# Attention masks written into PSUM by TensorE's four row groups, in place of masked maxima, minima and selects on the other engines

## What is computed

```
scores = einsum('bhqd,bhkd->bhqk', Q, K) / sqrt(16)
scores = where(mask, scores, -inf)       # a mask per layer, below
attn   = softmax(scores); out = einsum('bhqk,bhkd->bhqd', attn, V) @ Wo
```

## Time and profile before

| | |
|---|---|
| median of 3 runs | 1161.6 us (1161.47 to 1162.02) |
| profiled execution: device time | 1159.94 us |
| profiled execution: span | 1157.7 us |
| TensorE (PE) busy | 1106.9 us, 96% |
| VectorE (DVE) busy | 841.3 us, 73% |
| ScalarE (ACT) busy | 618.6 us, 53% |
| GpSimd (POOL) busy | 258.8 us, 22% |

### The profile page before, as it was taken

One profiled execution on the slowest core, in us unless ns is written; L12 is line 12 of the kernel. 1 busy time (PEld: TensorE's weight loads), 2 busy tenths in 40 slices (PEclk: granted clock), 3 DMA queues, 4 the chain that ended last, 5 costly groups with the idle time before them and its releaser, 6 DMA issues. The chain is left out here.

```text
span 1157.7 us, 36414 instructions
## 1 busy us (share of the span) xinstructions
PE 1106.9 (96%) x13908; PEld 921.1 (80%) x13908; DVE 841.3 (73%) x3468; ACT 618.6 (53%) x1584; POOL 258.8 (22%) x383
## 2 busy tenths in 40 slices
PE   6999999999999999999999999999999999999886
PEld 5878778888778788878888887888888878787665
DVE  4466987957878687697687777786778685987841
ACT  3644455455555556545556565655556455545453
POOL 0322412203121230222304032320321223121100
PEclk9999999999999999999999999999999999999997
DMA  9600010200111001010010202001010100110000
GB/s 339 246 11 2 2 48 11 84 20 2 28 40 28 39 16 52 2 41 26 16 52 2 66 2 66 2 16 52 16 52 2 52 2 2 52 47 7 2 6 10
DMA packets 21224, 45.11 MB, mean 39 GB/s; under 512 B 2496, under 2 KB 14912, under 8 KB 18112
## 3 DMA queue, kind: packets, MB, share of 16 engines
q1 hardware_dynamic: 19952, 41.36, 10.1%
q10 hardware_dynamic: 1104, 1.44, 0.4%
HBM read 40.70 MB, written 2.10 MB: 37 GB/s over the span
## 5 line engine op out<-in xcount | busy, mean ns | idle before, releaser
L663 POOL TENSOR_TENSOR root<-var_eps,halves 128x1 f32<-128x1 f32 x128 | 76.9, 602 | 609.9 <-DVE var_eps L1171 588.1
L971 ACT ACTIVATE exps_t<-bank 128x512 f32<-128x512 f32 x256 | 135.7, 605 | 34.3 <-PE bank L795 33.8
L1111 DVE CUSTOM_DVE_ANT_0 bank<-bank,bias 128x128 f32<-128x128 f32 x512 | 130.1, 324 | 18.8 <-PE bank L763 18.8
L721 PE MATMUL bank<-x_t,weights_A 128*128 128x128 f32 x1024 | 139.3, 284 | 2.7 <-ACT x_t L931 2.1
L721 PEld LDWEIGHTS bank<-x_t,weights_A 128*128 128x128 f32 x1024 | 127.3, 197 | 12.1 <-ACT x_t L931 4.5
L721 PE MATMUL bank<-x_t,weights_F 128*128 128x128 f32 x1024 | 127.9, 281 | 2.8 <-ACT x_t L931 1.7
L721 PEld LDWEIGHTS bank<-x_t,weights_F 128*128 128x128 f32 x1024 | 121.6, 195 | 9.1 <-ACT x_t L931 3.1
L808 PE MATMUL bank<-exps_t,v_one 128*32 128x128 f32 x3072 | 114.5, 277 | 8.2 <-DVE exps_t L1083 6.1
L714 PE MATMUL bank<-weights_F,exps_t 128*128 128x256 f32 x512 | 121.1, 383 | 0.2 <-DVE neg_max L1111 0.2
L763 PE MATMUL bank<-k_eo,q_t 32*128 32x256 f32 x1536 | 107.7, 396 | 2.6 <-issue 1.7
L1111 DVE DVE_READ_ACCUMULATOR2_ANT neg_max<- 128x1 f32 x768 | 106.5, 139 | 0.1
(11 more groups left out here) (112 smaller groups left out, 1964.8 us busy)
## 6 DMA issues: line engine op xcount, KB each, us to landing
weight<-in_fside SPq DMA_DIRECT2D x16, 1024.0 KB, 4.9
weights_A<-in_weights_A SPq DMA_DIRECT2D x4, 1028.0 KB, 15.3
weights_F<-in_weights_F SPq DMA_DIRECT2D x2, 2054.0 KB, 17.9
drop_raw<-in_drop SPq DMA_DIRECT2D x16, 256.0 KB, 5.3
x_hat<-in_x SPq DMA_DIRECT2D x16, 128.0 KB, 2.5
out<-x_sum SPq DMA_DIRECT2D x16, 128.0 KB, 1.7
ctx_t<-in_ctx_t SPq DMA_DIRECT2D x13, 128.0 KB, 3.0
rows_A<-in_rows_A SPq DMA_DIRECT2D x3, 512.0 KB, 15.4
```

The lines of the kernel that those rows point to most:

```text
L663: nc.gpsimd.tensor_tensor(root[x][:], var_eps[x][:], halves[:, e:e + 1], ALU.pow).then_inc(done["root"], 1)
L721: mm = nc.tensor.matmul(dst[:, 128 * f:128 * f + 128], w[:, c, 128 * f:128 * f + 128], tokens_t[:, c, :], start=(c == 0), stop=(c == KC - 1))
L971: nc.scalar.activation(dst, score_bank(x, "ST", s, j)[:], ACT.Exp, scale=DH ** -0.5).then_inc(done["exp"], 1)
L1111: ins = nc.vector.tensor_tensor_reduce(out=heads[:, n, :], in0=heads[:, n, :], in1=mask_bias(x, s), scale=-1.0, scalar=2.0 ** 126, op0=ALU ...
```

## The change

1. A new step `put_mask` writes a mask into four PSUM banks ahead of the scores: 16 bfloat16 products, 4 blocks of 32 mask rows times the 4 row groups, each with a 32 by 32 identity repeated for the 4 heads (128 columns). It stands ahead of both S and ST in A0, A2 and A5: 6 times per item. The mask rows lie in `causal_rows`, `pair_rows` (2 buffers, one raw buffer) and `sxs_rows`, each spread so that every row group has all four blocks.
2. A0's S also gets the key mask by four products of 512 columns, as A1 has it; both now read one tile `key_rows` for all items.
3. The masked maxima (L1111), the minima (L1083) and the select (L645) are gone: all stages take a plain maximum of four heads at once (the old L1116), and the product with V waits for the exponential alone.
4. At the start TensorE spreads the causal mask by 32 small products, which VectorE copies. x is loaded in the order of its first use, half of it from ScalarE's queue; a 256 KB broadcast of the key mask is replaced by a small tile. The item masks are loaded by eight transfers per item in place of two. The raw shared mask borrows the buffer of A3's byte mask, so the first load of A3's weights waits until VectorE has made `sxs_rows` (at F0's fold).
5. All order tables, PLACES included, are new.

```diff
-PRELOADED = {"S": ("A1",), "ST": ()}
-ADDED = ("A0", "A2", "A5")
+PRELOADED = {"S": ("A0", "A1", "A2", "A5"), "ST": ("A0", "A2", "A5")}
...
-12345112112332124001001124551111001122210200010202203000120100001023032323103000230330303010011011201124101000001221
...
+12435112212124110021100430022203111122220001100003403041212050201010210345204142411101444411554215415541521555000400
...
             def _(sp):
-                load_x(sp, 0)
+                for x in FIRST[::2]:
+                    load_x(sp, x)
                 load_keys(sp)
...
+                sp.wait_ge(sxs_made, 1)
+                load_weight(sp, WEIGHT_TURNS[0])
...
             def _(pe):
-                pe.wait_ge(const_made, 4)
+                pe.wait_ge(const_made, 5)
+                for a in range(4):
+                    for r, (by_key, left, right) in enumerate(((0, idb, causal), (1, causal, idb))):
+                        for j in range(GROUPS):
+                            mm = nc.tensor.matmul(banks[r][32 * j:32 * j + 32, 128 * a:128 * a + 128], left[:, 32 * a:32 * a + 32],
+                                                  right[:], start=True, stop=True)
+                mm.then_inc(causal_spread, 1)
+                pe.wait_ge(causal_made, 2)
...
+                    if s in ("A0", "A1"):
+                        pe.wait_ge(keys_made, 2)
+                        for j in range(GROUPS):
+                            nc.tensor.matmul(score_bank(x, "S", s, j)[:], idb[group_rows(j), 32 * j + x:32 * j + x + 1].broadcast_to([32, N]),
+                                             key_rows[group_rows(j), :].unsqueeze(1).broadcast_to([32, GH, N]), start=True, stop=True,
+                                             skip_group_check=True)
+                    if s in PRELOADED["ST"]:
+                        put_mask(x, "S", s, s != "A0")
...
+                def put_mask(x, kind, s, first):
+
+                    if s == "A5":
+                        pe.wait_ge(sxs_made, 1)
+                    elif s == "A2":
+                        pe.wait_ge(done["pairs"], nth(x, "pairs", "in"))
+                    rows_of = mask_rows(x, s, 1 if kind == "S" else 0)
+                    for a in range(4):
+                        for j in range(GROUPS):
+                            columns = score_bank(x, kind, s, j)[:].rearrange("p (n k) -> p n k", n=GH)[:, :, 32 * a:32 * a + 32]
+                            nc.tensor.matmul(columns, rows_of[group_rows(j), a, :],
+                                             idb[group_rows(j), 32 * j:32 * j + 32].unsqueeze(1).broadcast_to([32, GH, 32]),
+                                             start=(first and a == 0), stop=True, skip_group_check=True)
...
                 def outputs(x, s, j):
-                    made = "later" if s == "A0" else "keep" if s in ("A2", "A5") else "exp"
-                    pe.wait_ge(done[made], nth(x, made, s, j))
+                    pe.wait_ge(done["exp"], nth(x, "exp", s, j))
...
+                def pair_masks(x):
+
+                    dve.wait_ge(pairs_loaded, 128 * (PAIR_TURNS.index(x) + 1))
+                    if x >= PAIR_BUFFERS:
+                        dve.wait_ge(done["ST"], nth(x - PAIR_BUFFERS, "ST", "A2"))
+                    nc.vector.tensor_scalar(pair_rows[x % PAIR_BUFFERS][:], pair_raw[:], 0.0, MASKED, ALU.is_equal, ALU.mult
+                                            ).then_inc(done["pairs"], 1)
...
                 def group_max(x, s, j):
...
-                        for n in range(GH):
-
-                            ins = nc.vector.tensor_tensor_reduce(
-                                out=heads[:, n, :], in0=heads[:, n, :], in1=mask_bias(x, s), scale=-1.0,
-                                scalar=2.0 ** 126, op0=ALU.add, op1=ALU.min, accum_out=neg_max[x][:, j, n:n + 1])
-                        ins.then_inc(done["max"], 1)
-                        return
                     nc.vector.tensor_reduce(neg_max[x][:, j, :], heads, AX_X, ALU.max, negate=True
                                             ).then_inc(done["max"], 1)
```

More of the change, by code:

```diff
@@ L155, in vector_lane @@
                 yield "k_eo", ATTN[s]["feeds"]
-            if s in ("A2", "A5"):
-                yield from (("keep", s, j) for j in range(GROUPS))
             if ATTN[s]["feeds"] and ATTN[ATTN[s]["feeds"]]["b"]:
@@ L192, in pool_lane @@
     for s in STAGES:
-        if s == "A0":
-            yield from (("later", s, j) for j in range(GROUPS))
         for n in LNS_AFTER[s]:
@@ L331 @@
 OUT_AT, OUT_BEFORE = shared_places(OUT_PLACES, [b for b in SCALAR_ORDER if b[1] == "o_raw"])
+FIRST = [beat[0] for beat in TENSOR_ORDER if beat[1:] == ("xT", "A0") and beat[0] < SETS]
+PAIR_TURNS = [beat[0] for beat in SYNC_ORDER if beat[1] == "load_pairs"]
 WEIGHT_TURNS = [beat[0] for beat in SYNC_ORDER if beat[1] == "load_weight"]
@@ L450, in program @@
         first_loaded = sem("first_loaded")
-        pairs_loaded = [sem(f"pairs_loaded{x}") for x in range(PAIR_BUFFERS)]
+        pairs_loaded = sem("pairs_loaded")
+        keys_made = sem("keys_made")
+        causal_spread = sem("causal_spread")
+        causal_made = sem("causal_made")
         stored = sems("stored")
@@ L455, in program @@
         done |= {k: sem(f"done_{k}") for k in ("x_t", "square", "v_copy", "k_copy", "q_t", "m_t", "exp", "o_raw", "o_t", "h_t")}
[L456 removed]
+        done |= {k: sem(f"done_{k}") for k in ("pairs", "folded", "k_eo", "v", "times", "lower", "max", "high_low", "o_norm", "sum",
                                                "stats", "x_hat")}
[L458 to L460 removed]
+        done |= {k: sem(f"done_{k}") for k in ("root", "res")}
         high_made = sem("high_made")
@@ L518, in taken @@
             return done[taker[0]], nth(x, *taker)
-        def four(ap):
-            return ap.unsqueeze(1).broadcast_to([128, GH, 128])
         def slots(j):
@@ L537, in head, with mask_rows @@
             return 8 * (n // 2) + 2 * j + n % 2
-        def mask_bias(x, s):
-            m = ATTN[s]["mask"]
-            return sxs_bias[:] if m == 3 else bias[x][:, m, :]
+        def mask_rows(x, s, by_key):
+            masks = causal_rows if s == "A0" else sxs_rows if s == "A5" else pair_rows[x % PAIR_BUFFERS]
+            return masks[:, by_key]
         def whole(name, b):
@@ L779, in transposed_scores @@
                         return
+                    masked = s in PRELOADED["ST"]
+                    if masked:
+                        for j in range(GROUPS):
+                            free_bank((x, "ST", s), j)
+                        put_mask(x, "ST", s, True)
                     for n in range(GH):
                         for j in range(GROUPS):
-                            if n == 0:
+                            if n == 0 and not masked:
                                 free_bank((x, "ST", s), j)
                             mm = nc.tensor.matmul(score_bank(x, "ST", s, j)[:, 128 * n:128 * n + 128], k_eo[x][group_rows(j), n // 2, n % 2, :],
-                                                  q_t[x][group_rows(j), n // 2, :], start=(n == 0), stop=True,
+                                                  q_t[x][group_rows(j), n // 2, :], start=(n == 0 and not masked), stop=True,
                                                   skip_group_check=True)
@@ L922, in _ @@
                 act.dma_start(weights["A0"][:, 0:half], dram["weights_A0"][:, 0:half]).then_inc(first_loaded, 16)
+                for x in FIRST[1::2]:
+                    load_x(act, x)
                 act.dma_start(weights["A0"][:, half:], dram["weights_A0"][:, half:]).then_inc(stage_loaded["A0"], 16)
-                for x in range(3):
+                for x in FIRST[1::2]:
                     load_ctx(act, x)
@@ L1014, in _ @@
                                       ).then_inc(parity_made, 1)
+                dve.wait_ge(causal_spread, 1)
+                for r in range(2):
+                    nc.vector.tensor_copy(causal_rows[:, r].rearrange("p a n -> p (a n)"), banks[r][:]).then_inc(causal_made, 1)
+                dve.wait_ge(keys_loaded, 32)
+                nc.vector.tensor_scalar(key_rows[:], key_raw[:], 0.0, MASKED, ALU.is_equal, ALU.mult).then_inc(keys_made, 1)
+                nc.vector.tensor_scalar(key_cols[:], key_cols_raw[:], 0.0, MASKED, ALU.is_equal, ALU.mult).then_inc(keys_made, 1)
                 def fold_norm(x, s):
```

268 lines of the change are left out of this document (97 added, 171 removed).

## The result

| | before | after |
|---|---|---|
| median of the runs | 1161.6 us | 1144.95 us (1143.6 to 1147.0) |
| ratio after to before, 95% interval | | 0.9854 [0.9837, 0.987] |
| profiled execution: device time, span | 1159.94, 1157.7 us | 1147.0, 1145.2 us |

1.5% faster. I had forecast 0.4% slower, and the time lies under my range too.

The account below looks back on a forecast made before the run. TensorE, busy 96% of the span, was taken as the bound: 1159.94 + 29.3 us added work - 24.5 us recovered, plus 1.7 us from profile to median, gives 1166 us, 0.4% slower. Own range 1159 to 1175; 8-in-10 range 1149 to 1181.

Parts of the forecast that it names:

- The sum's first term: Work added on TensorE by 96 put_mask steps at 0.34 us each, taken from the shift step: 32.6 us.
- My lower bound: For one put_mask on TensorE: 0.22 us, since the key mask streams the same 2048 columns in that time.
- Entry price: First float32 step on row groups behind a full-array product costs about 0.1 us more; 6.8 us come back.
- My count of 107 and 39 steps: S and ST steps directly behind a full-array product: 107 before, 39 after; 68 x 0.1 us saved.
- Key masks: A0's key masks on TensorE, 16 times four products of 512 columns at 0.22 us: 3.5 us more.
- Middle: 80 to 1040 us: of TensorE's 20.4 us idle, 11 come back as VectorE is relieved; bounds 0 and 17.
- End: Last 117.7 us: 8 of 19.4 us idle come back, plus 3 us on the last F1 product's clock.
- Start: TensorE's 9.33 us wait for the first x: 2.5 us come back with lighter loads; bounds -1 and 4.
- A: Rival: relief of VectorE is larger than TensorE's added work, 38 us back, 1153 us; chance 0.31.
- B: Rival: A3's single weight buffer makes TensorE late by 3 us at each of five items, 1181 us; chance 0.06.
- C: Rival: mask products don't pack as the shift does, 0.50 us a step, 15 us more, 1181 us; chance 0.04.
- D: Rival: both sides cancel within 0.2% (2.3 us); 33 us come back or a put_mask costs 0.25 us; chance 0.19.

Follow-up runs that it names:

- e4: The changed kernel with the 16 products of each put_mask done twice: 1165.66 us, 1.0038 of before.
- e9: The changed kernel with a full-array product of zeros, one column, between each mask step and its S or ST: 1163.62 us, 1.0031 of before.
- e10: The changed kernel with a one-column product of zeros on 32 rows between each mask step and its S or ST: 1146.99 us, 0.9887 of before.
- e2: The kernel before with A0, A2 and A5 unmasked (plain maxima, no minima, no select), order tables unchanged: 1137.63 us, 0.9788 of before.
- e1: The changed kernel with the order tables and bank places of before, item masks made at F0: 1156.94 us, 0.9971 of before.
- e3: The changed kernel without its 96 put_mask steps (A2 and A5 unmasked, A0 with the key mask alone): 1128.72 us, 0.9717 of before.
- e7: The changed kernel with x loaded by SyncE alone, in the order of before: 1145.53 us, 0.9858 of before.
- e13: The changed kernel with 33 further bfloat16 products, results unused, in TensorE's empty first 9 us: 1140.79 us, 0.9824 of before.
- e14: The changed kernel unedited, on the same chip as e13: 1144.69 us, 0.9859 of before.

## Why the prediction was wrong

1. **The sum's first term, "96 x 0.34 = 32.6 us", failed.** A mask step holds TensorE 0.22 to 0.23 us: 22.3 us, summed from start to next start over all 96 (a recorded wait of 1.5 us inside one of them taken off). The shift that I took it from stood ahead of a full-array product, and a third of its time was for leaving the form; a mask step stands ahead of S or ST and leaves nothing (e4, e9, e10). My lower bound, the key mask at 0.22, was the right row: it stood ahead of S.
2. **Entry price.** Right as a thing, too small, and by another route: 6.8 us forecast, while S and ST together fell from 187.1 to 178.4 us, 8.7, recorded waits taken off. Each S or ST behind a mask fell by only 0.05 us (1.02 and 0.95, not 0.96 and 0.89). My count of 107 and 39 steps left out those behind a product with V, 35 before and 18 after, where S takes 1.08 us too. The rest are steps that no longer leave the form themselves, and waits that the records cover; these I can't separate.
3. **Key masks**, 3.5 us forecast; their sum rose from 4.3 to 7.1, 2.8 us. All work together: 22.3 + 2.8 - 8.7 = 16.4 us, where 29.3 were forecast. The runs agree: e2 to e1 gives 19.3 for about the same work, and e3 to after 16.2 for the masks without the key masks, where 25.8 were forecast. So 10 to 13 of the 21 us that I missed by are here.
4. **Middle, 11 us: the visible idle time fell by 2.0.** The relief alone took 8.1 us of it away in the old order (20.4 to 12.3 in e2); masks and new order put 6.1 back. The reading "all that can come back is idle time" failed: the relief in the old order gave 23.1 us, 9.2 of them in the busy time of the same products (4.3 of these at the products with V). I had named these waits and priced them at nothing. And VectorE's fall was read wrongly (270 us, in truth 156, overlapping records); the smaller fall gave more.
5. **End, 8 and 3 us.** Right mechanism; the first was too small, 13.2 us of idle time, and the second right, 2.8 us for the F1 product.
6. **Start, 2.5 us.** x did come sooner and 1.9 us of idle time went, but e7 shows no gain from it in the time. The number was near the idle time by luck: I had no price for projections that run slower when they start sooner.
7. **Rivals.** A came nearest; at 1153 us it was too high, as it kept the 29.3 us of work. B didn't happen: no wait at the weights in A3 stands among PE's larger ones (one of 0.6 us). C fell: a strided output and a new stationary operand each time cost nothing visible. D didn't happen, though its mask step of 0.25 us was near the measured 0.22 to 0.23; and I had worked it out wrongly. With 33 us back, or with 0.25 us a step, my own sum gives 1157.9 or 1157.8 us, 3.7 us under before and outside D's 2.3. Its band belongs to 27 to 31.6 us back, or 0.27 to 0.31 us a step.

The work came out under my lower bound (16.4 for 18), the recovery at about 33 of at most 40. My range left out that both lie at their good ends together, though one row, read at another place, would have decided the first.

## What to carry to other kernels

Read a short step's duration only where its neighbours are what they will be at the new place: from start to next start it contained here the price of leaving the array's form. Idle time isn't the most that relief can return: of e2's relief, 20.6 us by the profiled spans, 11.3 were idle time. Compare the same products' time from start to next start at places that wait for another engine and at places that don't. A half idle engine can still be on the path, if its results are needed at once: test it by doubling one of its steps, without a wait of its own. And before crediting a gain to the place of an edit, line up the two timelines and see where the lead arises.

## What the runs showed of the hardware

- 16 bfloat16 products of 32 rows and 128 columns in four row groups take 0.22 to 0.23 us, 14 ns each from start to start. The Trainium skill (TensorE: Matmul & The Clock Gate, section "Wait — 56ns, not 53.3ns?") has a floor of about 25 ns; the measurement decides, and on row groups in turn it is lower.
- A full-array product of one column between two steps on row groups costs 0.25 us in the trace: 0.09 more on the step ahead, 0.11 for itself, 0.05 more on the step behind (e9); in the time it is 18.7 / 96 = 0.19 us. On 32 rows the same product shows nothing of it (e10). The Trainium skill (TensorEngine Tiling (Array Packing), "Key Properties") says that a change of tiling mode drains TensorE; the trace fits this in that each change has a price, with these sizes; the draining itself no row shows.
- 33 products without use ahead of the program's first large ones took 3.9 us off 1144.7 (e13 to e14). The projections behind them took 4.16 us in place of 5.59; where the rest comes from is open.
